# Second layer of a two-layer recurrent block: decay differences as two float32r products of gates split into top bits and rest

## The reference

```python
g = -jnp.exp(A_log) * jax.nn.softplus(x @ Wa.T + dt_bias)     # log of the decay, <= 0
beta = jax.nn.sigmoid(x @ Wb.T)
def step(S, inputs):
    S = S * jnp.exp(g_t)[..., None, None]
    kv = jnp.einsum('bhk,bhkv->bhv', k_t, S)
    u = b_t[..., None] * (v_t - kv)
    S = S + jnp.einsum('bhk,bhv->bhkv', k_t, u)
    o_t = jnp.einsum('bhk,bhkv->bhv', q_t * scale, S)
```

## Time and profile before

| | |
|---|---|
| median of three runs | 1365.99 us (1365.13 to 1367.12) |
| span of the profiled execution | 1361.7 us |
| time of the profiled execution beside its span | not recorded separately |
| granted TensorE clock, mean | 0.995 |
| PE busy | 1315.0 us, 97% |
| DVE busy | 1063.5 us, 78% |
| ACT busy | 737.4 us, 54% |
| POOL busy | 528.7 us, 39% |

### The profile page before, as it was taken

One profiled execution on the slowest core, in us unless ns is written; L12 is line 12 of the kernel. 1 busy time (PEld: TensorE's weight loads), 2 busy tenths in 40 slices (PEclk: granted clock), 3 DMA queues, 4 the chain that ended last, 5 costly groups with the idle time before them and its releaser, 6 DMA issues. The chain is left out here.

```text
span 1361.7 us, 24113 instructions
## 1 busy us (share of the span) xinstructions
PE 1315.0 (97%) x8866; PEld 640.7 (47%) x8866; DVE 1063.5 (78%) x1855; ACT 737.4 (54%) x1307; POOL 528.7 (39%) x434
## 2 busy tenths in 40 slices
PE   5888999999999999999999999999999999999998
PEld 2333333333333333333344546855486555855475
DVE  7888978778877887788884985778776976868846
ACT  5675666556655666556657552455334652355431
POOL 3499953012211221112222763247431762328431
PEclk9998999999999999999999999999999999999999
DMA  6520000010000000000254024002311024001121
GB/s 232 190 81 8 7 9 3 15 41 14 9 17 32 24 7 7 24 30 15 87 196 184 20 52 82 25 24 60 51 44 40 8 71 82 17 32 43 34 46 47
DMA packets 80468, 68.50 MB, mean 50 GB/s; under 512 B 46080, under 2 KB 67296, under 8 KB 77792
## 3 DMA queue, kind: packets, MB, share of 16 engines
q1 hardware_dynamic: 67936, 65.39, 15.5%
q10 hardware_dynamic: 12416, 1.57, 1.1%
HBM read 44.87 MB, written 17.87 MB: 46 GB/s over the span
## 5 line engine op out<-in xcount | busy, mean ns | idle before, releaser
L621 DVE TENSOR_REDUCE mS<-vpair 128x1 f16<-128x512 f32 x512 | 329.1, 685 | 111.6 <-PE vpair L1125 109.5
L936 ACT ACTIVATE probs<-bank 128x512 f16<-128x512 f32 x512 | 277.1, 594 | 163.0 <-PE bank L1132 162.8
L1179 PE MATMUL bank<-rows,both 128*128 128x512 f16 x1024 | 243.0, 380 | 0.4 <-DVE th L650 0.3
L436 POOL TENSOR_TENSOR h<-th,h 128x512 f16<-128x512 f32 x61 | 71.4, 1171 | 213.2 <-ACT h L907 213.2
L1179 PEld LDWEIGHTS bank<-rows,both 128*128 128x128 f16 x1024 | 91.3, 98 | 121.2 <-issue 13.9
L2257 PE MATMUL bank<-rows,both 128*128 128x512 f16 x512 | 118.6, 382 | 0.0
L1125 PE MATMUL vpair<-qk 32*128 32x512 f16 x512 | 100.3, 387 | 13.1 <-DVE mS L621 7.7
L2273 PE MATMUL bank<-both,hid 128*128 128x512 f16 x512 | 111.2, 379 | 0.0
L2241 PE MATMUL bank<-rows,both 128*128 128x512 f16 (+1 forms) x456 | 104.0, 379 | 0.9 <-PEq L160 0.9
L1132 PE MATMUL bank<-qv,qk 32*128 32x512 f16 x512 | 99.7, 386 | 0.0
L1193 PE MATMUL bank<-dn,h 128*128 128x512 f16 x256 | 98.0, 383 | 0.0
(11 more groups left out here) (363 smaller groups left out, 2654.1 us busy)
## 6 DMA issues: line engine op xcount, KB each, us to landing
h<-in_ug SPq DMA_DIRECT2D x8, 1024.0 KB, 5.5
lt_scratch<-big SPq DMA_DIRECT2D x16, 384.0 KB, 2.7
dn<-in_down SPq DMA_DIRECT2D x2, 2048.0 KB, 11.1
x_scratch<-th SPq DMA_DIRECT2D x16, 256.0 KB, 2.2
res<-x_scratch SPq DMA_DIRECT2D x16, 256.0 KB, 4.3
out_x<-res SPq DMA_DIRECT2D x16, 256.0 KB, 2.0
both<-in_w SPq DMA_DIRECT2D x2, 1548.0 KB, 10.4
t_scratch<-tok SPq DMA_DIRECT2D x16, 192.0 KB, 2.1
```

The lines of the kernel that those rows point to most:

```text
L436: pool.tensor_tensor(h16(ft, 1), row32, h16(ft, 0), ALU.subtract).then_inc(S["row_lo"], 1)
L621: v.tensor_reduce(mS[:, u % 2, qt, 32 * j + DH:32 * j + DH + 1], SA[n % 2][:, :], AX.X, ALU.max).then_inc(S["max_done"], 1)
L936: a.activation(probs[:, n % (2 * G), :], SB[n % 2][:, :], ACT.Exp, scale=float(DH) ** -0.5).then_inc(S["p_ready"], 1)
L1179: mm = pe.matmul(GB[n % 2][:, :], w[:, kt, col:col + P], xnb(b, kt), start=r == 0, stop=r == 2 * KT - 1)
```

## The change

The gates are split into two float32 parts: the word of each gate with its lowest 12 bits cleared (`gs[:, 0]`), and the rest (`gs[:, 1]`, the difference), both on DVE, which adds two 24-column instructions per batch. POOL's `spread(tt)` forms gU from each part, in a tensor of its own of type float32r, with two slots for tt and two parts each, so two instructions for one. The constant `after` is copied once into a float32r tensor by DVE, in batch 0 behind gg. On PE each product of the differences becomes two, of the type float32r, accumulated in the same bank: four matmuls in the program per tt where two stood. The smaller DMA scratch makes room for the new tensors.

```diff
+TOP_BITS = -(1 << 12)
...
-        GT, gU = (big[:, 10], big[:, 12]), (big[:, 11], big[:, 13])
+        GT = big[:, 10], big[:, 12]
+        gU = sb("gU", [P, 2, 2, LH, P], F32R)
+        after_r = sb("after_r", [P, P], F32R)
+        gs = sb("gs", [P, 2, TT, LH])
...
                         pool.wait_ge(S["a_full"], AI[b, "DT", tt - 2, 1] + 1)
-                    pool.wait_ge(S["g_r"], b + 1)
-                    pool.tensor_tensor(gU[tt % 2], over(upto, LH), hb(gg[:, tt, :], P), ALU.mult).then_inc(S["gU_r"], 1)
+                    for i in range(2):
+                        pool.wait_ge(S["gs_r"], b * 2 + i + 1)
+                        pool.tensor_tensor(gU[:, tt % 2, i], over(upto, LH), hb(gs[:, i, tt, :], P), ALU.mult).then_inc(S["gU_r"], 1)
...
                 v.tensor_tensor(gg, spl, negA[:, :].rearrange("p (t c) -> p t c", t=1).to_broadcast([P, TT, LH]),
                                 ALU.mult).then_inc(S["g_r"], 1)
+                if b == 0:
+                    v.wait_ge(W["x1_last"], 32)
+                    v.tensor_copy(after_r[:, :], after).then_inc(S["after_ready"], 1)
+                v.wait_ge(S["g_r"], b + 1)
+                v.tensor_scalar(gs[:, 0].bitcast(I32), gg.bitcast(I32), TOP_BITS, None, ALU.bitwise_and).then_inc(S["gs_r"], 1)
+                v.wait_ge(S["gs_r"], b * 2 + 1)
+                v.tensor_tensor(gs[:, 1], gg, gs[:, 0], ALU.subtract).then_inc(S["gs_r"], 1)
...
                 def differences(tt):
+                    if b == 0 and tt == 0:
+                        pe.wait_ge(S["after_ready"], 1)
                     for hf in range(2):
                         bk = afill("DT", tt, hf)
-                        pe.wait_ge(S["gU_r"], b * TT + tt + 1)
-                        pe.matmul(bk[:, 0:HH * P], after, gU[tt % 2][:, hf:LH:2, :], start=True, stop=True).then_inc(S["a_full"], 1)
+                        pe.wait_ge(S["gU_r"], (b * TT + tt + 1) * 2)
+                        pe.matmul(bk[:, 0:HH * P], after_r[:, :], gU[:, tt % 2, 0, hf:LH:2, :], start=True, stop=False)
+                        pe.matmul(bk[:, 0:HH * P], after_r[:, :], gU[:, tt % 2, 1, hf:LH:2, :], start=False, stop=True).then_inc(S["a_full"], 1)
...
-    nc = bacc.Bacc("TRN2", target_bir_lowering=False, num_devices=1)
+    nc = bacc.Bacc("TRN2", target_bir_lowering=False, num_devices=1, dynamic_dma_scratch_size=512)
```

More of the change, by code:

```diff
@@ L6 @@
 F16 = mybir.dt.float16
+F32R = mybir.dt.float32r
 I32 = mybir.dt.int32
@@ L1442, in layer1 @@
             "dve": ["v_took", "kv_took", "st_r", "mv_r", "rs0_r", "xs_r", "xh_r", "xl_r", "conv", "sil_r", "beta_r", "az_r",
-                    "spl_r", "g_r", "small_r", "gcs_r", "kS_r", "V2_r", "ssS_r", "oss_r", "or_r", "y_r", "fd_r", "g2_r",
+                    "spl_r", "g_r", "gs_r", "after_ready", "small_r", "gcs_r", "kS_r", "V2_r", "ssS_r", "oss_r", "or_r", "y_r", "fd_r", "g2_r",
                     "out_r", "snm_r", "ls_r", "sub", "wo_r"],
```

## The result

The changed kernel takes 1384.24 us (median of 4 runs, 1382.26 to 1384.63), the kernel before 1366.55 (1365.13 to 1368.22) beside it: a ratio of 1.0135 with a 95% interval of 1.0122 to 1.0149. It is 17.7 us slower; 1380 was predicted, in a range of 1363 to 1390.

What follows compares the result with a forecast made beforehand. PE, DVE and POOL were taken to run level in 28 us of each batch, where the edit adds work. Lateness of 13.4 us plus 1 for the clock on 1366.0 gave 1380.4, called 1380; range 1363 to 1390.

Steps and rivals of the forecast that it cites:

- Turns between DVE and POOL: First gU block: four turns of 1.87 us instead of two, so silu(2) and squares(2) come 2.8 us late.
- Rival B: POOL's serial time counts but DVE hardly waits: 1369 us, or 1372 with half the DVE delay; chance 0.22.
- Three small operations behind conv(7): On DVE, one to two of them wait up to 1.9 us; its first KQ take is 3.4 to 4.9 us late.
- e5: Small DVE tensor_scalar behind conv(7), ahead of the first KQ take; one of three, of which one to two wait 1.9 us.
- PE's saving: differences(tt) holds PE 0.65 us instead of 1.29, 10.2 us less over 16 tiles.
- Lateness per batch: When the up tiles begin: 3.3 us (2.4 to 4.4) in three batches, 3.5 in b=0, sum 13.4.
- Clock: New PE waits of 2 us and more invite a fall of the granted clock: 0 to 5.2 us, taken as 1.
- Rival A: All added work is hidden and PE's 0.64 us x 16 come through: 1356 us; chance 0.13.
- D: On PE, float32r runs no faster than fp32, four products of 0.64 us per tile: 1395 us; chance 0.07.
- C: The waits halve the clock each time, twice per batch outside DVE's cover: 1390 us; chance 0.08.
- The bookkeeping: On DVE ahead of conv(3): gs[0] and gs[1] take 0.18 us each, with the semaphores 0.4 us per batch.

Runs made afterwards that it cites:

- memset: The changed kernel with POOL's second gU replaced by two memsets of 768 columns, PE reading the first part twice: 1368.55 us, ratio 1.0013.
- fill: The changed kernel with idle float16 matmuls in PE's three new waits of every batch (4, 10 and 8): 1379.34 us, ratio 1.0099.
- pool: The changed kernel with fp32 products as before; POOL still forms a second gU, which nothing reads: 1384.08 us, ratio 1.0134.
- book: The kernel before plus only the new buffers, the copy and the two DVE operations; one gU, fp32 products: 1367.81 us, ratio 1.0017.
- pe: The changed kernel with POOL forming only the top part's gU, which all four float32r products read: 1363.46 us, ratio 0.9989.
- late: The changed kernel with DVE's four small instructions moved behind the KQ takes of tile 0: 1395.51 us, ratio 1.0224.

## Why the prediction was right, and where a size was off

- **Turns between DVE and POOL.** Right. silu(2) ends 2.92 us later behind gg than before (predicted 2.8), squares(2) start 2.93 us later behind vec (2.8). memset shows that this is the cause: POOL nearly as long, 15.2 of the 17.7 us gone. Rival B (POOL's serial time only, 1369 to 1372) had squares(2) late as well, so that its 2.23 us wait doesn't tell the two apart. B fails on DVE's rows (conv(3) 5.71 us, silu(2) 1.95 us and 2.92 us late) and on the time, and memset (1368.55) is what B would look like. The Trainium skill (SBUF — State Buffer, Who interferes with whom) says "fully blocks", which the prediction quotes, of VectorE's 2-port modes; of an instruction with two SBUF inputs it says only that it contends with one that reads. The size of a turn (about 1.9 us) is known from the earlier trace rows alone.
- **Three small operations behind conv(7).** I had one or two held for up to 1.9 us. In the changed kernel's b=1 all three are, and take 1.1 to 1.3 us each. In fill, where the clock doesn't blur it, two are (sn 1.32 and sn5 1.39 us, e5 0.12), and DVE's first KQ take starts 30.87 us behind vec (943.31 less 912.44), before 26.46 (934.09 less 907.63): 4.4 us late, inside the 3.4 to 4.9 forecast.
- **PE's saving.** The products start 0.25, 0.17, 0.17 and 0.18 us apart, 0.77 us a tile for 0.65 predicted: the first of four has 0.08 more, which I had not counted, and the others 0.17 where I had 0.163. The saving is 0.52 us x 16 = 8.3 and not 10.2. As forecast most of it went into waits and differences(3) gave its part back, 0.6 us per batch by pool and fill; the medians of pool without the saving and the changed kernel with it, 1384.08 and 1384.24, hide this behind the clock. The Trainium skill (FP8 and Floating Point Precision, TensorE Precision Notes) counts four passes for fp32 and names a reduced form that truncates, without its number of passes. If float32r is that form, the trace fits one pass: 0.17 us for a product that took 0.64.
- **Lateness per batch.** Predicted 3.3 in b=1 to 3 and 3.5 in b=0, 13.4 in all. With the clock held up (fill) it is 3.49, 3.47, 3.48 and 3.46, 13.9 in all.
- **Clock.** The term that was mis-sized. I took 1 us out of 0 to 5.2, arguing that most falls lie beside DVE's chain. That holds for b=0, whose later waits absorb it (47.64 us, fill 47.74). In the others PE has work without a gap from pre_tile(6) up to pairs("KK", 1), and DVE, gapless before, now has idle time too (in b=1 0.21 us ahead of conv(6), 0.37 ahead of its first KK take). The falls add 1.33 us in b=1, 2.91 in b=2 (two) and 1.32 in b=3. Measured: 19.4 - 13.9 = 5.5 in the traces, 3.4 to 4.9 in the medians. That is the 4 us between 1380 and 1384.
- **Rival A** (all hidden, 1356) and **D** (float32r as slow as fp32) are out by the rows above. **C** (1390, clock twice per batch) had the clock's falls right in kind, but at too large a price: five falls show in the trace, four of which cost.
- **The bookkeeping.** 0.4 us per batch forecast for the two gs operations; book shows them at 0.18 us each and 0.56 us per batch on the path.

## What to carry to other kernels

Before giving an idle POOL more work, look at what DVE does at that moment. Here a DVE without gaps feeds PE, and two more gU instructions (1.47 us each when nothing holds them) cost DVE 2.5 us in conv(3) and silu(2). Neither merging the instructions nor shifting small operations past them bought it back. Work that only writes cost 2.5 us in all where the reading work cost 17.7, and with the second gU on ACT 5.4 to 7.7 us of the loss were left. A microsecond off PE is worth nothing just ahead of a wait on those engines, however near 100% its busy share stands. And price a new PE wait of 2 us together with the matmuls behind it: in the changed kernel each fall of the clock in b=1 to 3 took a further 1.3 to 1.5 us.

## What was not expected of the hardware

- The clock fell in pe as well, behind a wait of only 1.11 us (4.45 us for pre_tile(6)), but not behind the same place's 1.23 us in memset or 2.22 us in late, b=1 (2.76 us each); in late it fell 25 us later. Where it falls is not settled by the length of the one wait in front; these runs don't tell what else decides.
- A memset on POOL holds a 24-column tensor_scalar: in memset, b=1, sn5 runs beside the second memset (933.07 to 933.81) and takes 0.47 us, 933.37 to 933.84, where it took 0.24. The two-input sn, at 933.15 beside the same memset, takes 0.18 us.
- Activations of 128 columns with a float32r output go 0.3 us apart (12 in 3.60), so 768 columns in six pieces (1.85 us in act) cost ACT nearly what one gU costs POOL with DVE in its way (1.91 us).
